# Attention scores as whole-array products over stacked rows, in a reordered turn, with query copies on ScalarE's queue

## The reference

```python
scores = jnp.einsum('bhnd,bhmd->bhnm', Q, K) / jnp.sqrt(jnp.float32(D))
scores = jnp.where(mask == 0, -jnp.inf, scores)
attn = jax.nn.softmax(scores, axis=-1)
out = jnp.einsum('bhnm,bhmd->bhnd', attn, V)
```

## Time and profile before

| | |
|---|---|
| Time, median of 3 runs | 1268.31 us |
| Lowest and highest | 1262.6 and 1273.34 us |
| Span of the profiled execution | 1276.2 us |
| TensorE busy | 1203.0 us, 94% |
| VectorE busy | 998.5 us, 78% |
| ScalarE busy | 786.4 us, 62% |
| GpSimd busy | 673.1 us, 53% |
| Mean granted TensorE clock | 0.969 of full speed |

### The profile page before, as it was taken

How to read it: one execution, slowest core, us unless ns; L and a number is a source line. 1 busy time by engine, 2 the same in 40 slices (tenths; PEclk the granted TensorE clock), 3 DMA queues, 4 the chain that set the end, 5 groups by cost and what they waited for, 6 DMA issues and landing times.

```text
span 1276.2 us, 27021 instructions
## 1 busy us (share of the span) xinstructions
PE 1203.0 (94%) x9168; PEld 1111.4 (87%) x9169; DVE 998.5 (78%) x2077; ACT 786.4 (62%) x1521; POOL 673.1 (53%) x772
## 2 busy tenths in 40 slices
PE   7999999989888999999799999999999999899998
PEld 6888888879878999999788888888899998788887
DVE  6888888866797676666668888887887788878887
ACT  4777677658554555555557767776444445677874
POOL 5333333333104555553777777730465466778885
PEclk8999999979899999999869999999999999999999
DMA  3221112023201333333533333302100000000000
GB/s 104 62 61 53 51 51 51 19 66 108 75 1 38 114 107 103 108 104 97 123 65 64 60 63 60 60 23 84 38 2 0 0 0 1 2 25 25 25 25 33
DMA packets 72319, 68.67 MB, mean 54 GB/s; under 512 B 26624, under 2 KB 64256, under 8 KB 72000
## 3 DMA queue, kind: packets, MB, share of 16 engines
q1 hardware_dynamic: 57936, 47.78, 12.5%
q0 software_dynamic: 12576, 18.62, 7.9%
q10 hardware_dynamic: 1744, 1.50, 0.4%
HBM read 44.00 MB, written 18.61 MB: 49 GB/s over the span
## 4 chain that ended last, share of the span: by engine, by line
PE 73%; DVE 10%; issue 7%; ACT 5%; POOL 4%; DMA 0%; ACTq 0%; DVEq 0%; POOLq 0%
PE PSUM L772 13%; PE PSUM L774 13%; PE PSUM L773 12%; PE PSUM L832 6%; PE PSUM L853 6%; PE PSUM L841 4%; PE PSUM L785 3%; PE PSUM L851 2%; PE PSUM L808 2%; PE PSUM L862 2%; POOL s_t_gh L2614 2%; PE PSUM L1914 1%; DVE s_a_q_lo L422 1%; ACT s_a_q_hi L677 1%; PE PSUM L2803 1%
## 5 line engine op out<-in xcount | busy, mean ns | idle before, releaser
L2164 POOL TENSOR_TENSOR s_f_h_lo<-s_f_h,s_f_h_hi 128x512 fp32r<-128x512 f32 x64 | 93.4, 1466 | 104.6 <-ACT s_f_h_hi L2108 104.0
L1337 POOL DMA_INDIRECT s_m_tile_x<-normed_x,s_tokens x78 | 95.7, 1227 | 77.0 <-DVE s_tokens L1628 55.5
L853 PEld LDWEIGHTS PSUM<-s_a_v_diagonal,s_a_prob_t 128*128 128x128 f32 x1024 | 128.4, 195 | 0.0
L853 PE MATMUL PSUM<-s_a_v_diagonal,s_a_prob_t 128*128 128x36 f32 x1024 | 127.4, 271 | 0.0
L1005 POOL DMA_INDIRECT s_x<-sorted_y,s_slots x60 | 95.1, 1586 | 50.2 <-DMA s_x<-sorted_y,s_slots 34.0
L454 DVE TENSOR_REDUCE s_a_row_max<-PSUM 128x8 f32<-128x640 f32 x128 | 104.4, 815 | 12.9 <-PE PSUM L832 10.3
L702 ACT ACTIVATE s_a_prob_t<-PSUM 128x640 f32<-128x640 f32 x128 | 89.4, 699 | 34.2 <-PE PSUM L841 33.4
L832 PE MATMUL PSUM<-s_a_kd,s_a_q_hi 64*128 64x320 f32 x512 | 92.8, 366 | 16.7 <-DVE s_a_q_lo L422 16.7
L461 DVE TENSOR_TENSOR s_a_less<-PSUM,s_a_row_max 128x640 f32<-128x640 f32 x128 | 105.0, 820 | 3.6 <-issue 0.2
L685 ACT ACTIVATE s_a_prob<-s_a_less 128x512 f32<-128x512 f32 x128 | 80.5, 629 | 41.8 <-DVE s_a_less L461 41.7
L2102 ACT ACTIVATE s_f_h<-PSUM,s_cols 128x512 f32<-128x512 f32 x64 | 44.0, 688 | 89.0 <-PE PSUM L774 88.3
(11 more groups left out here) (327 smaller groups left out, 4318.4 us busy)
## 6 DMA issues: line engine op xcount, KB each, us to landing
sorted_y<-s_m_tile_y SPq DMA_DIRECT2D x39, 256.0 KB, 2.1
s_a_kd<-s_a_k_parts SPq DMA_DIRECT2D x252, 20.0 KB
s_x<-x SPq DMA_DIRECT2D x16, 256.0 KB, 2.8
s_a_ctx<-ctx SPq DMA_DIRECT2D x32, 128.0 KB, 2.5
s_moe_raw<-moe_w SPq DMA_DIRECT2D x16, 256.0 KB, 3.4
normed_x<-s_m_xn SPq DMA_DIRECT2D x16, 256.0 KB, 3.2
y<-s_x SPq DMA_DIRECT2D x16, 256.0 KB, 2.1
s_late_raw<-moe_w SPq DMA_DIRECT2D x11, 256.0 KB, 2.8
```

What stands on the lines that cost most here:

```text
L853: last = pe.matmul(a.o_ps[:, 2 * c:2 * c + 2, :], a.prob_t[j % 2][:, c, :], v[:, j // BT, 0, 2 * c:2 * c + 2], start=False, stop=c == PC - ...
L1337: pool.indirect_dma_start(m.tile_x[n % 2][:, t, :], None, d["normed_x"], bass.IndirectOffsetOnAxis(ap=tokens[:, BT * n + t:BT * n + t + 1] ...
L2164: pool.tensor_tensor(f.h_lo[m % 4][:], f.h[m % 4][:], f.h_hi[m % 4][:].bitcast(F32), ALU.subtract).then_inc(f.h_split, 1)
```

## The change

The scores of a unit become four products, one for each pair of heads, over 96 rows: three stacks of 32 rows (two heads of 16 channels) that hold queries hi, lo, hi and, opposite them, keys hi, hi, lo. The three products of the split are thereby summed inside one product of 160 columns. The weights and biases of queries and keys are reordered on the host (`by_pair`) so that row 4r + p of a chunk belongs to pair p. New copies build the stacks: `stack_rounded_queries` sends q_hi twice from ScalarE's DMA queue and `stack_queries` sends q_lo once from SyncE's, 256 KB each; `spread_keys` sends six copies of 40 KB. `q_hi` and `q_lo` become single buffers, and one semaphore pair, `stacks_in`, counts all nine copies of a block.

```diff
+HEAD_PAIRS = HPC // 2
+PAIR_ROWS = 2 * HD
+STACK = 3 * PAIR_ROWS
+STACK_DMAS = 3 * 2 + 3
...
+    row = np.arange(P) // 4
+    chunk_order = (2 * (np.arange(P) % 4) + row // HD) * HD + row % HD
+    by_pair = np.concatenate([m * P + chunk_order for m in range(KC)])
...
-                self.q_hi = [sb(scope, n + f"q_hi{z}", [P, KC, SEQ], F32R) for z in two]
-                self.q_lo = [sb(scope, n + f"q_lo{z}", [P, KC, SEQ], F32R) for z in two]
-                self.k_parts = [sb(scope, n + f"k_parts{z}", [P, 2, KC, CTXP], F32R) for z in two]
...
+                self.q_hi = sb(scope, n + "q_hi", [P, KC, SEQ], F32R)
+                self.q_lo = sb(scope, n + "q_lo", [P, KC, SEQ], F32R)
...
+                    self.q_stack = [sb(scope, n + f"q_stack{z}", [P, HEAD_PAIRS, KC, SEQ], F32R) for z in two]
...
-        def spread_keys(engine, a, b, heads):
+        def spread_keys(engine, a, b, places):
             engine.wait_ge(a.k_split, b.count + 1)
-            for h in heads:
-                rows = slice(h * HD, (h + 1) * HD)
-                engine.dma_start(a.kd[b.z][rows, :, :, h % (HPC // 2), :].bitcast(F32),
-                                 a.k_parts[b.z][rows].bitcast(F32)).then_inc(a.kd_in[b.z], 16)
+            for h in places:
+                for copy, part in enumerate((0, 0, 1)):
+                    rows = slice(copy * PAIR_ROWS + h * HD, copy * PAIR_ROWS + (h + 1) * HD)
+                    engine.dma_start(a.kd[b.z][rows, h].bitcast(F32),
+                                     a.k_parts[b.z][h * P // 2:(h + 1) * P // 2, part].bitcast(F32)).then_inc(a.stacks_in[b.z], 16)
+
+        def stack_queries(engine, a, b):
+            stack = a.q_stack[b.z]
+            engine.wait_ge(a.q_split, b.count + 1)
+            engine.dma_start(stack[PAIR_ROWS:2 * PAIR_ROWS].bitcast(F32), a.q_lo[:].bitcast(F32)).then_inc(a.stacks_in[b.z], 16)
+
+        def stack_rounded_queries(act, a, b):
+            act.wait_ge(a.q_round, b.count + 1)
+            for copy in (0, 2):
+                act.dma_start(a.q_stack[b.z][copy * PAIR_ROWS:(copy + 1) * PAIR_ROWS].bitcast(F32),
+                              a.q_hi[:].bitcast(F32)).then_inc(a.stacks_in[b.z], 16)
```

VectorE's turn:

```diff
             def body(b, behind, ahead):
                 late_rows = a.stage == 1 and not behind
-                if ahead and (a.stage or behind):
-                    ln_apply(b.next())
                 if a.stage and ahead == 0:
                     ffn_norm(0)
+                score_max(b, 1)
                 if behind:
                     normalise(b.last(), 2)
-                score_max(b, 1)
                 less_max(b, 1)
+                if ahead:
+                    x_residue(b.next())
                 if ahead > 1 and not late_rows:
                     ln_stats(b.next().next())
                 if a.stage and ahead == 1:
                     ffn_stats()
                 if a.stage and ahead == 0:
                     ffn_norm(1)
-                if ahead:
-                    keys(b.next())
-                if ahead:
-                    value_tails(b.next())
                 if behind:
                     normalise(b.last(), 3)
+                score_max(b, 2)
+                less_max(b, 2)
+                normalise(b, 0)
+                if ahead:
+                    q_residue(b.next())
                 if ahead > 1 and not late_rows:
                     ln_aggregate(b.next().next())
                 if a.stage and ahead == 1:
                     ffn_aggregate()
-                score_max(b, 2)
-                less_max(b, 2)
-                normalise(b, 0)
-                if ahead:
-                    x_residue(b.next())
+                score_max(b, 3)
                 if behind:
                     o_residue(b.last())
-                score_max(b, 3)
+                if ahead > 1:
+                    keys(b.next().next())
+                less_max(b, 3)
+                if ahead:
+                    value_tails(b.next())
+                if a.stage and ahead == 0:
+                    ffn_residue()
+                normalise(b, 1)
                 if late_rows:
                     ln_stats(second.next())
                     ln_aggregate(second.next())
                 if ahead:
-                    q_residue(b.next())
-                less_max(b, 3)
-                if a.stage and ahead == 0:
-                    ffn_residue()
-                if ahead:
                     score_max(b.next(), 0)
-                normalise(b, 1)
-                if ahead:
                     less_max(b.next(), 0)
                 if behind:
                     residual(b.last())
+                if ahead > 1:
+                    ln_apply(b.next().next())
 
```

ScalarE: the waits of three functions, and its turn:

```diff
             def keys_rounded(b):
                 if opens(a, b):
-                    act.wait_ge(first_steps, 2)
+                    act.wait_ge(a.first_k_ps, 1)
+                elif isinstance(b.n, int) and b.n == 0:
+                    act.wait_ge(a.v_ps, b.count + 1)
+                elif isinstance(b.n, int) and b.n == 1:
+                    act.wait_ge(a.first_k_ps, 2 + a.stage)
                 else:
-                    act.wait_ge(a.kv_ps, b.count + 1)
-                after(act, a.kd_in[b.z], 16 * HPC * (b.half + a.base // 2))
+                    act.wait_ge(a.v_ps, b.count)
+                after(act, a.stacks_in[b.z], 16 * STACK_DMAS * (b.half + a.base // 2))
                 for m in range(KC):
...
-            def values(b):
-
-                act.wait_ge(a.k_split, b.count + 1)
-                if opens(a, b):
-                    act.wait_ge(a.kv_ps, 1)
+            def values(b, keys_split):
+
+                act.wait_ge(a.v_ps, b.count + 1)
+                after(act, a.k_split, keys_split)
...
+                if not (isinstance(b.n, int) and b.n == 0):
+                    stacked = b.last()
+                    act.wait_ge(a.stacks_in[stacked.z], 16 * STACK_DMAS * (stacked.half + a.base // 2 + 1))
```

```diff
             def body(b, behind, ahead):
+                exponential(b, 0)
                 if behind:
                     transposed(b.last(), 3)
-                exponential(b, 0)
                 mask_laid(b, 2)
                 if ahead:
-                    keys_rounded(b.next())
+                    x_rounded(b.next())
+                transposed(b, 0)
                 exponential(b, 1)
-                if ahead:
-                    values(b.next())
-                transposed(b, 0)
                 mask_laid(b, 3)
                 if ahead:
-                    x_rounded(b.next())
+                    q_rounded(b.next())
                 exponential(b, 2)
-                transposed(b, 1)
+                if ahead:
+                    stack_rounded_queries(act, a, b.next())
+                if ahead:
+                    mask_laid(b.next(), 0)
                 if behind:
                     o_rounded(b.last())
+                transposed(b, 1)
+                if ahead > 1:
+                    keys_rounded(b.next().next())
                 if ahead:
-                    q_rounded(b.next())
-                    mask_laid(b.next(), 0)
+                    values(b.next(), b.count + 3 if ahead > 1 else 0)
+                exponential(b, 3)
+                if ahead:
+                    mask_laid(b.next(), 1)
                 transposed(b, 2)
                 if ffn_tokens and not ahead:
                     ffn_tokens()
-                exponential(b, 3)
-                if ahead:
-                    mask_laid(b.next(), 1)
-
```

TensorE: the scores, the waits of `project`, and its turn, whose end is as before (weigh_values(b, 1), score(b.next(), 0), project(b.last())):

```diff
             def score(b, j):
                 u = UNITS * b.count + j
                 m, qt = j // BT, j % BT
-                pe.wait_ge(a.kd_in[b.z], 16 * HPC * (b.half + a.base // 2 + 1))
-                pe.wait_ge(a.q_split, b.count + 1)
+                if j == 0:
+                    pe.wait_ge(a.stacks_in[b.z], 16 * STACK_DMAS * (b.half + a.base // 2 + 1))
                 pe.wait_ge(a.masked, u + 1)
-                queries = (a.q_hi[b.z], a.q_lo[b.z], a.q_hi[b.z])
-                keys = (a.kd_hi[b.z], a.kd_hi[b.z], a.kd_lo[b.z])
-                for i in range(3):
-                    for c in range(2):
-                        rows = slice(c * P // 2, (c + 1) * P // 2)
-                        ps = a.scores[:, j % 2, c, 0:HPC // 2 * CTXP].rearrange("p (h n) -> p h n", n=CTXP)
-                        last = pe.matmul(ps, queries[i][rows, m, qt * P:(qt + 1) * P], keys[i][rows, m],
-                                         start=False, stop=i == 2, skip_group_check=True)
+                for p in range(HEAD_PAIRS):
+                    ps = a.scores[:, j % 2, p // 2, p % 2 * 2 * CTXP:(p % 2 + 1) * 2 * CTXP].rearrange("p (h n) -> p h n", n=CTXP)
+                    last = pe.matmul(ps, a.q_stack[b.z][0:STACK, p, m, qt * P:(qt + 1) * P], a.kd[b.z][0:STACK, :, p, m, :],
+                                     start=False, stop=True, skip_group_check=True)
                 last.then_inc(a.scores_ps, 1)
...
                 if ahead:
```

(30 more changed lines are left out.)

128 lines of the change are left out of this document (80 added, 48 removed).

## The result

| | us | share of before |
|---|---|---|
| before, median of 4 runs | 1265.49 | |
| after, median of 4 runs (1417.38 to 1421.3) | 1419.38 | 1.1203, 95% interval 1.1159 to 1.1247 |
| forecast | 1256 (1236 to 1281) | |

The kernel became 12% slower, 154 us, where 12 us less was forecast. The page of the changed kernel: busy time, the 40 slices, the chain that ended last, the costliest group and the DMA issues.

The account below looks back on a forecast made before the run. Attention turns were taken as nearly all TensorE work, 15.5 us, becoming a 15.0 us hand-over loop: 27 turns save 13.5, less 2 at stage starts, plus 0.5 at ends, 12 us off, giving 1256 us (range 1236 to 1281).

Parts of the forecast that it names:

- The copies: Query copies between queries and next block's first score: each 256 KB taken to land in 3.4 us, hidden.
- cover: Time from the residues' copy issue at 2.6 us to 6.9 us, within which copies stay hidden: 4.3 us.
- The copies land late: Rival: copies landing beyond 4.3 us hold up the next block's first score; put at 1289 us, chance 0.12.
- the clock falls: Rival: new TensorE waits drop the granted clock three more times, 12 off becoming 15 on, 1283 us; chance 0.10.
- The loop of hand-overs: Attention turn: TensorE, VectorE and ScalarE tied through the one PSUM bank `misc`, closing at 15.0 us.
- both waits: TensorE in each turn: 0.3 us for q_split ahead of the keys, 0.7 us for value tails ahead of the projection.
- ScalarE's issues: Two DMA issues a turn on ScalarE, 0.45 us each, costing nothing but leaving no cover over.
- Keys sent a turn ahead: Key copies of block b+2 on SP's queue, sent a whole turn ahead of use.
- The new products: Score group on TensorE: four products of 160 columns, 0.12 us each, 0.47 a group, against 0.63 before.
- TensorE's work without waits: Attention turn after the change: 13.9 us of TensorE work, four score groups saving 1.1 us.
- The term for the stage ends: Attention stages: about 1 us lost at each of two starts; shorter scores give about 0.5 us in last turns.
- The first rival: TensorE alone sets the turn, as the two waits mostly don't occur: about 14.2 us a turn, 1235 us; chance 0.15.

Follow-up runs that it names:

- all 128 partitions: Changed kernel with the same three query copies each written to all 128 partitions, scores using a constant tile: 1267.03 us, ratio 0.9989.
- the filled wait: Changed kernel with the value products ahead of the next block's first score run three times in place of once: 1397.9 us, ratio 1.0982.

## Why the prediction was wrong

**What failed: the landing of the copies.** The step "The copies" took 3.4 us, with 2.1 and 5.9 as its ends, against cover of 4.3. Measured are 6.7 us for the residues, outside the bounds, though the cover was right to 0.1 us (4.2). Two terms were missing.
- The rate. The rows behind 3.4 and 2.1 are of transfers that use all 128 partitions. Into 32 neighbours the three copies and the weight chunk took 6.9 us, with the DMA engines fully busy, against 3.5 to 4.1 into a wider stretch. The Trainium skill (SBUF — State Buffer, Door 1: The DMA port swizzle) has this rule, and the prediction weighed it, but one copy at a time, with 1.2 us added to rows of one transfer. Measured, a first copy takes 1.4 us and each behind it 2.1.
- The queue. Each copy was costed as if alone. The copies share the same 16 engines, and their packets ran one copy after the other; the residues, which TensorE waits for, were sent last of the three and carry the time of the two in front. Even with the prediction's 1.2 us a copy the sum goes over the cover. As an estimate with the 1.2 us to the first packet and the 1.4 us to the signal measured here: 1.2 + 3 x 1.2 + 1.4, less the 1.45 us by which ScalarE's first copy is issued ahead, is 4.8 us. With the measured 1.4, 2.1 and 2.1 it is 6.7. The weight chunk stands behind the residues and delays nothing.

Neither term alone would have lengthened the turn: three copies at the high rate cost nothing (all 128 partitions), nor did one at the low rate in the first stage (14.87 us). The prediction's count of bytes, 768 KB more a turn, also leaves out 80 KB of key copies (six of 40 KB for eight of 20), which changes nothing in this.

**The rival was named and too small.** "The copies land late" put 5.9 us at 1300 and decided from 5.2 on. At 6.7 its own rule gives a turn of about 17.4, 50 us over before and some 1320. The turns that ran at full clock with the copies as they are (the filled wait) took just that, 17.4. The rest is the other rival, "the clock falls", which was put apart from it at 0.10: with a wait of 3.2 us in every turn the lower clock comes in nearly every turn, 3.0 us each in the first stage. The two weren't independent. In the traces 24 of the turns (blocks 3 to 15 of each stage) account for 124 of the 154 us that the changed kernel takes over the one without copies; 33 are lost at the openings, above all the first, and 4 come back behind attention. Before's trace had the sign: one fall after a wait of 0.92 us.

**What was right.** The loop of hand-overs, 14.85 measured for 15.0, with both waits at their places (0.2 and 0.63 for 0.3 and 0.7). ScalarE's issues cost nothing of note. Keys sent a turn ahead never held up a score. The new products: 0.12 us apart at full clock, 0.49 us a group for 0.47.

**What was mis-sized beside it.** TensorE's work without waits is 14.2 us and not 13.9, hidden by the loop. The term for the stage ends was -2 and +0.5. A group of 64-row products also costs 0.1 us behind it, which the forecast left out. The openings took 13 us, at the second stage more by the lower clock than by the longer waits, so that even without the copies the medians are only 2.3 and 6.5 us under before. Why TensorE's clock stays low there for longer isn't settled, and the table of the openings rests on one trace of each kernel. The first rival (TensorE alone, 14.2 a turn) didn't occur.

## What to carry to other kernels

Here SBUF-to-SBUF copies that fold 128 partitions into 32 or 64 neighbours ran at about half the rate; where the layout is free, interleave the copies' rows over the partitions (three slices gave 138 us here). Cost copies in bursts, not one by one: all that the shared engines still have to move when a copy is issued stands in front of it. A wait of some us added to every turn of such a loop had two prices here, itself and the clock after it, and a gain in the steady turns has to be set against the turns that open each stage.
